# Two attentions of a fused transformer block: the spread reciprocal goes through a PSUM bank, by_block moves to GpSimd, and the first maxima read unstacked halves

## The reference, cut to what matters

```
a = softmax(einsum('bhsd,bhtd->bhst', q, k) * D ** (-0.5))
if causal:
    a = a * (arange(t)[None, :] > arange(s)[:, None])
o = einsum('bhst,bhtd->bhsd', a, v)
```

## Time and profile before

| | us |
|---|---|
| median of 3 runs | 3939.13 (3935.78 to 3939.37) |
| the profiled execution | 3941.99 |
| its span | 3940.2 |
| PE busy | 3361.1 (85%) |
| DVE busy | 2602.9 (66%) |
| ACT busy | 1943.1 (49%) |
| POOL busy | 1420.3 (36%) |

### The profile page before, as it was taken

How to read it: one execution, slowest core, us unless ns; L and a number is a source line. 1 busy time by engine, 2 the same in 40 slices (tenths; PEclk the granted TensorE clock), 3 DMA queues, 4 the chain that set the end, 5 groups by cost and what they waited for, 6 DMA issues and landing times. The chain is left out here.

```text
span 3940.2 us, 64014 instructions
## 1 busy us (share of the span) xinstructions
PE 3361.1 (85%) x22007; PEld 1491.6 (38%) x22007; DVE 2602.9 (66%) x4846; ACT 1943.1 (49%) x3897; POOL 1420.3 (36%) x716
## 2 busy tenths in 40 slices
PE   5999999519885998998989895888889898869998
PEld 2323322307762232322322263222222222657776
DVE  6888885581116778787787355777777773555665
ACT  2777787231112456575566542355555556423443
POOL 2000000452221432414324231366565667506453
PEclk7989998657986999999999796899999999969999
DMA  1000000386752100001000021100000000437445
GB/s 57 14 12 10 12 8 3 148 319 209 227 186 62 32 6 17 13 9 25 5 9 5 24 83 37 31 7 17 14 17 11 8 9 1 128 104 261 89 83 116
DMA packets 163206, 238.92 MB, mean 61 GB/s; under 512 B 35859, under 2 KB 132826, under 8 KB 155994
## 3 DMA queue, kind: packets, MB, share of 16 engines
q1 hardware_dynamic: 142698, 209.40, 16.8%
q0 software_dynamic: 19056, 24.88, 3.5%
q10 hardware_dynamic: 1152, 0.79, 0.1%
HBM read 136.44 MB, written 68.92 MB: 52 GB/s over the span
## 5 line engine op out<-in xcount | busy, mean ns | idle before, releaser
L1254 DVE TENSOR_REDUCE a_part_max<-a_wb 128x1 f32<-128x512 f32 (+1 forms) x2048 | 1164.7, 625 | 268.9 <-PE a_wb L1335 257.8
L1190 ACT ACTIVATE a_e<-a_sc 128x512 f32<-128x512 f32 (+1 forms) x1472 | 796.8, 599 | 785.8 <-PE a_sc L1360 778.3
L1335 PE MATMUL a_wb<-a_ks,a_qs 96*128 96x512 f16 (+1 forms) x2048 | 762.8, 383 | 120.0 <-DVE a_part_max L1254 101.0
L1148 POOL TENSOR_TENSOR a_part_sum<-a_part_sum,a_e 128x2048 f32<-128x2048 f32 x160 | 724.2, 4527 | 185.4 <-ACT a_e L1190 170.0
L1360 PE MATMUL a_sc<-a_qs,a_ks 97*128 97x512 f16 (+1 forms) x1472 | 559.4, 395 | 11.9 <-DMA a_qs<-a_neg_max 8.0
L748 DVE TENSOR_REDUCE xa_part_max<-xa_mx 128x2 f32<-128x802 f32 x512 | 469.7, 985 | 103.8 <-PE xa_mx L845 102.8
L692 ACT ACTIVATE xa_e<-xa_sc 128x512 f32<-128x512 f32 (+1 forms) x832 | 445.7, 596 | 114.2 <-PE xa_sc L832 106.3
L1335 PEld LDWEIGHTS a_wb<-a_ks,a_qs 96*128 96x128 f16 x2048 | 203.2, 99 | 752.0 <-DVE a_part_max L1254 558.8
L1383 PE MATMUL a_po<-a_e,a_v 128*32 128x512 f32 (+1 forms) x2432 | 334.3, 622 | 2.3 <-ACT a_dc L1160 1.2
L1137 POOL TENSOR_TENSOR a_em<-a_e,a_later 128x512 f32<-128x512 f32 x64 | 81.0, 1266 | 590.3 <-issue 371.2
L868 PE MATMUL xa_po<-xa_e,xa_v 128*32 128x256 f32 (+1 forms) x3328 | 274.0, 402 | 7.5 <-ACT xa_oc L735 2.6
(11 more groups left out here) (359 smaller groups left out, 4500.7 us busy)
## 6 DMA issues: line engine op xcount, KB each, us to landing
experts_w_up<-in_we SPq DMA_DIRECT2D x32, 1024.0 KB, 6.2
wall<-expert_halves SPq DMA_DIRECT2D x18, 1088.0 KB, 7.2
experts_w_down<-in_we SPq DMA_DIRECT2D x32, 512.0 KB, 6.3
a_qs<-a_stage SPq DMA_DIRECT2D x360, 32.0 KB, 1.9
moe_xr<-sorted_rows SPq DMA_DIRECT2D x79, 136.5 KB, 2.1
a_ks<-a_stage SPq DMA_DIRECT2D x336, 32.0 KB, 1.9
choose_whole<-in_wm SPq DMA_DIRECT2D x18, 544.0 KB, 9.0
expert_halves<-choose_cut SPq DMA_DIRECT2D x18, 544.0 KB, 7.8
```

The lines of the kernel that those rows point to most:

```text
L1148: pool.tensor_tensor(part_sum[:, :, :], part_sum[:, :, :], tile, ALU.add).then_inc(pool_added, 1)
L1190: act.activation(e[:r, m % ering, j, :], sc[(HG * m + j) % NSC][:r, :], ACT.Exp, scale=scale).then_inc(exp_done, 1)
L1254: dve.tensor_reduce(part_max[:, j, t, k:k + 1], src[:, :mxw], AX.X, ALU.max).then_inc(unit_taken, 1)
L1335: last = pe.matmul(dst[:, :mxw], qs[:STACK, j, n % NQ, P * t:P * t + P], ks[:STACK, g % 2, j, mxs[k]:mxs[k] + mxw], start=True, stop=True)
```

## The change

Four things are edited, all in `attention_stacked`.

- "norm" becomes a numbered unit and gets a `wb` bank: the spread reciprocal is transposed into PSUM, and the multiplication reads it there. PE skips the unit but leaves it the bank.
- In windows with passed tiles, "total" moves to index 20 and "carry" to index 33, and the transposition of `dc` and the addition move from "norm" to "carry". The addition reads the carried sum straight from its bank, and the copy to `divisor` goes.
- `by_block` is written by POOL (`place_sums`), at the fifth tile of the next window.
- The first 16 maxima of window 0 read the high halves in `stage` (32 rows), without the stacking DMAs. Value block 0 stands in the middle of these, block 1 in the middle of the next 16, and blocks 2 and 3 behind the turn.

```diff
@@ -985,12 +985,13 @@
-    before = [("k", 0, 0), ("q", 0), ("k", 0, 1)] + [("v", 0, b) for b in range(nvb)]
+    before = [("k", 0, 0), ("q", 0), ("k", 0, 1)]
     for i in range(nmx):
-        before += maxima(0, [i]) + ([("k", 0, i + 2)] if i + 2 < len(kch) else [])
+        span = maxima(0, [i])
+        before += span[:8] + ([("v", 0, i)] if i < 2 else []) + span[8:] + ([("k", 0, i + 2)] if i + 2 < len(kch) else [])
         if i == 1:
             before.append(("q", 1))
-    before.append(("turn", 0))
+    before += [("turn", 0)] + [("v", 0, b) for b in range(2, nvb)]
...
             work[34:34] = [("norm", n - 1)]
             if passed(n - 1, 0):
-                work[22:22], work[28:28] = [("total", n - 1)], [("carry", n - 1)]
+                work[20:20], work[33:33] = [("total", n - 1)], [("carry", n - 1)]
...
-    number = {u: i for i, u in enumerate(u for u in order if u[0] not in ("total", "norm"))}
+    number = {u: i for i, u in enumerate(u for u in order if u[0] != "total")}
+    ready_at = {u: i for i, u in enumerate(u for u in order if u[0] not in ("total", "norm"))}
...
+            def place_sums(n):
+
+                pool.wait_ge(total_ready, carry_at[n] + 1)
+                if carry_at[n]:
+
+                    pool.wait_ge(unit_ready, ready_at[("carry", max(k for k in carry_at if k < n))] + 1)
+                pool.tensor_tensor(by_block[:, :, :, :],
+                                   total[:, :, :].rearrange("p t j -> p j t").unsqueeze(3).to_broadcast([P, HG, TPC, TPC]),
+                                   in_block[:, :].unsqueeze(1).unsqueeze(1).to_broadcast([P, HG, TPC, TPC]),
+                                   ALU.mult).then_inc(blocks_ready, 1)
+
             for n in range(NC if causal or own_sum else 0):
...
                 for kt in range(nkt):
+                    if kt == TPC and n - 1 in carry_at:
+                        place_sums(n - 1)
...
+            if NC - 1 in carry_at:
+                place_sums(NC - 1)
...
             def carry_sums(n):
 
-                if carry_at[n] == 0:
-                    dve.wait_ge(mask_filled, 5)
+                if carry_at[n]:
+
+                    dve.wait_ge(blocks_ready, carry_at[n])
                 dve.wait_ge(exp_done, HG * (nkt * n + TPC * (n % NCH)))
...
-                dve.tensor_tensor(by_block[:, :, :, :],
-                                  total[:, :, :].rearrange("p t j -> p j t").unsqueeze(3).to_broadcast([P, HG, TPC, TPC]),
...
             def take(u):
-                if u[0] != "norm":
-                    i = number[u]
-                    src = wb[i % NWB]
+                i = number[u]
+                src = wb[i % NWB]
...
-                elif u[0] == "carry":
-                    dve.wait_ge(unit_ready, i + 1)
-                    dve.tensor_copy(divisor[:, :], src[:, :HG * TPC]).then_inc(unit_taken, 1)
-                elif u[0] == "norm":
+                elif u[0] in ("carry", "norm"):
                     n = u[1]
+                    steps = sum(4 if k in carry_at else 3 for k in range(n))
+                    den = turned[:, :].rearrange("p (b r) -> p b r", r=SLOT)[:, :, 0]
+                    if u[0] == "carry" or n not in carry_at:
+                        dve.wait_ge(o_taken, NCOPY * (n + 1))
+                        dve.transpose(turned[:, :], dc[:, :]).then_inc(norm_step, 1)
+                        dve.wait_ge(norm_step, steps + 1)
+                    if u[0] == "carry":
+                        dve.wait_ge(unit_ready, ready_at[u] + 1)
+                        dve.tensor_tensor(divisor[:, :], den, src[:, :HG * TPC], ALU.add).then_inc(norm_step, 1)
+                        dve.wait_ge(norm_step, steps + 2)
+                        dve.sem_inc(unit_taken, 1)
+                        return
...
+                    dve.reciprocal(inverse[:, :], den).then_inc(norm_step, 1)
+                    dve.wait_ge(norm_step, steps + 2)
+                    if i >= NWB:
+
+                        dve.wait_ge(unit_taken, i - NWB + 1)
+                    dve.transpose(src[:, :].rearrange("p (b r) -> p b r", r=SLOT), over(inverse[:, :], SLOT)).then_inc(norm_step, 1)
+                    dve.wait_ge(norm_step, steps + 3)
                     g, o = n // NCH, CH * (n % NCH)
...
-                        dve.tensor_tensor(divisor[:, :], divisor[:, :], den, ALU.add).then_inc(norm_step, 1)
...
-                    dve.transpose(turned[:, :].rearrange("p (b r) -> p b r", r=SLOT), over(inverse[:, :], SLOT)).then_inc(norm_step, 1)
-                    dve.wait_ge(norm_step, steps + 2)
-                    dve.tensor_tensor(ot[:, g, o:o + CH], oc[:, :], turned[:, :], ALU.mult).then_inc(divided, 1)
+                    dve.tensor_tensor(ot[:, g, o:o + CH], oc[:, :], src[:, :], ALU.mult).then_inc(divided, 1)
+                    dve.wait_ge(divided, n + 1)
+                    dve.sem_inc(unit_taken, 1)
...
                     g = n // NCH
-                    if (t, j) == (0, 0):
+                    straight = (n, k) == (0, 0)
+                    if (t, j) == (0, 0) and straight:
+                        pe.wait_ge(split_ready, max(staged[("q", 0)], staged[("k", 0, 0)]) + 1)
+                    elif (t, j) == (0, 0):
                         wait_stacked(pe, ("q", n))
...
+                    if straight:
+                        rows = slice(SLOT * j, SLOT * j + SLOT)
+                        last = pe.matmul(dst[:, :mxw], stage[rows, staged[("q", 0)] % NST, 0, P * t:P * t + P],
+                                         stage[rows, staged[("k", 0, 0)] % NST, 0, :mxw], start=True, stop=True)
+                    else:
+                        last = pe.matmul(dst[:, :mxw], qs[:STACK, j, n % NQ, P * t:P * t + P],
+                                         ks[:STACK, g % 2, j, mxs[k]:mxs[k] + mxw], start=True, stop=True)
```

More of the change, by code:

```diff
@@ L1204, in carry_sums @@
                 dve.wait_ge(total_ready, carry_at[n] + 1)
-                if carry_at[n]:
-                    dve.wait_ge(unit_ready, number[("carry", max(k for k in carry_at if k < n))] + 1)
-                dve.tensor_tensor(by_block[:, :, :, :],
-                                  total[:, :, :].rearrange("p t j -> p j t").unsqueeze(3).to_broadcast([P, HG, TPC, TPC]),
-                                  in_block[:, :].unsqueeze(1).unsqueeze(1).to_broadcast([P, HG, TPC, TPC]),
-                                  ALU.mult).then_inc(blocks_ready, 1)
             def take(u):
-                if u[0] != "norm":
-                    i = number[u]
-                    src = wb[i % NWB]
+                i = number[u]
+                src = wb[i % NWB]
                 if u[0] in "kq":
@@ L1259, in take @@
                     n = u[1]
-                    g, o = n // NCH, CH * (n % NCH)
-                    dve.wait_ge(o_taken, NCOPY * (n + 1))
-                    dve.transpose(turned[:, :], dc[:, :]).then_inc(norm_step, 1)
-                    steps = sum(4 if k in carry_at else 3 for k in range(n)) + 1
-                    dve.wait_ge(norm_step, steps)
-                    den = turned[:, :].rearrange("p (b r) -> p b r", r=SLOT)[:, :, 0]
-                    if n in carry_at:
-                        dve.wait_ge(unit_taken, number[("carry", n)] + 1)
-                        dve.tensor_tensor(divisor[:, :], divisor[:, :], den, ALU.add).then_inc(norm_step, 1)
-                        steps += 1
-                        dve.wait_ge(norm_step, steps)
-                        den = divisor[:, :]
@@ L1272, in take @@
-                    dve.reciprocal(inverse[:, :], den).then_inc(norm_step, 1)
-                    dve.wait_ge(norm_step, steps + 1)
-                    dve.transpose(turned[:, :].rearrange("p (b r) -> p b r", r=SLOT), over(inverse[:, :], SLOT)).then_inc(norm_step, 1)
-                    dve.wait_ge(norm_step, steps + 2)
-                    dve.tensor_tensor(ot[:, g, o:o + CH], oc[:, :], turned[:, :], ALU.mult).then_inc(divided, 1)
+                    steps = sum(4 if k in carry_at else 3 for k in range(n))
@@ new lines, in take @@
+                    if n in carry_at:
+                        den, steps = divisor[:, :], steps + 1
+                    dve.reciprocal(inverse[:, :], den).then_inc(norm_step, 1)
[4 more added lines that the diff above has]
+                    dve.wait_ge(norm_step, steps + 3)
@@ L1334, in unit @@
                                     wait_stacked(pe, ("k", g, c))
-                    last = pe.matmul(dst[:, :mxw], qs[:STACK, j, n % NQ, P * t:P * t + P],
-                                     ks[:STACK, g % 2, j, mxs[k]:mxs[k] + mxw], start=True, stop=True)
+                    if straight:
[5 more added lines that the diff above has]
+                                         ks[:STACK, g % 2, j, mxs[k]:mxs[k] + mxw], start=True, stop=True)
                 elif u[0] == "carry":
```

## The result

| | before | after | ratio (95% interval) |
|---|---|---|---|
| median, us | 3939.25 (4 runs, 3935.78 to 3940.26) | 3850.22 (4 runs, 3843.78 to 3858.91) | 0.9777 (0.9756 to 0.9798) |
| profiled execution: span, us | 3940.2 | 3842.0 | |

The change takes 89 us off the median and 98 us off the profiled execution. The predicted 3820 was 30 us too low; 3850 lies in the range (to 3870), but above the likeliest case's own (3797 to 3845).

What follows compares the result with a forecast made beforehand. PE was taken to set the pace in both loops, DVE close behind. Gaps 68, clock 46, starts 5.5 and ends 1 made 120 us off 3941.99: 3822, given as 3820, with a range to 3870.

Steps and rivals of the forecast that it cites:

- the likeliest case: The whole sum with the clock mostly back: 3797 to 3845 us, chance 0.66.
- The bound, and the multiplication: PE sets the pace in both loops; norm's multiplication, freed of POOL by PSUM, takes 0.69 us: 39.1 us less in a2.
- The bank: At norm, PE can make two maxima instead of three while DVE divides, but goes on a reduction earlier: counted as nothing.
- The chain cut in two: In ten a1 windows, moving transposition and addition to carry shrinks norm's gap from 1.36 to about 0.4 us: 10 us.
- the addition's 9.0: In a1's loop, 10 additions to the divisor fall from 10.9 to 1.9 us: 9.0 us less.
- The clock: In both loops, most PE time at half level outside gaps returns to full: 46 us, between 0 and 63.
- The starts: First reductions come earlier in each attention: 2 us in a1 and 3.5 in a2, together 5.5, between 0 and 9.
- The ends: Behind a1's loop the transposition and the copy leave the last chain: 1 us.
- POOL did not come late: Rival: POOL, inside sums, is late with by_block and PE stands at 12 carries: 3950 us, chance 0.03.
- cover for POOL's sums: Rival: the loops' gaps had let POOL catch up, so half the gain is lost: about 3880 us, chance 0.06.
- the clock would not come back: Rival: remaining gaps in the loops keep bringing half level, clock gain 0 to 20 us: 3845 to 3865, chance 0.2.
- the footing: The sum's 3822 us stood against the profiled execution, 3 us over the median; 3819 on the median's footing, 3820 said.

Runs made afterwards that it cites:

- e1: The changed kernel with the spread reciprocal in SBUF again, so the multiplication has two SBUF inputs: 3915.9 us.
- e2: The kernel before with only the numbered norm and the multiplication reading the spread reciprocal from PSUM: 3878.6 us.
- e9: The changed kernel with the spread reciprocal in SBUF and norm taken out of the count of banks: 3907.8 us.
- e4: The changed kernel with carry directly ahead of norm, so DVE's chain in a1 is whole again: 3857.9 us.
- e5: The changed kernel with two extra transpositions of the inverse in each norm, a longer pause without any lock: 3935.8 us.
- e6: The changed kernel with by_block written by DVE again instead of POOL: 3856.4 us.
- e11: The changed kernel, unchanged, measured once more: 3848.3 us.
- e3: The kernel before with the new start alone (first maxima from unstacked halves, value blocks moved): 3934.9 us.
- e7: The changed kernel with the denominators' transposition and the reciprocal done ahead of norm, or at carry where there is one: 3825.0 us.
- e8: The changed kernel with the queries' projection moved from among the maxima to directly behind norm: 3827.1 us.

## Why the prediction was right, and where it was off

**The bound, and the multiplication.** Right: 0.69 us, least and most alike, with POOL in a sum. e1 shows that nothing else does it. The Trainium skill's rule of the exclusive lock (SBUF — State Buffer, "SBUF: two separate sides"), that a VectorE instruction with two SBUF inputs and GpSimd shut each other out of the ports that they share, agrees: 3294 ns with two SBUF inputs, 687 with one, in otherwise the same program. `a2`'s gaps fell by 35.4 us (34.6 in e2) for the 39.1 forecast. 1.6 us are left at each "norm", the upper of the two values that the prediction worked out, 1.4 and 1.6; the sum was made with the more favourable view that all of DVE's saving reaches PE. The transposition into PSUM cost 727 ns for 711.

**The bank, "I take nothing".** Nearly right: at most some 6 us (e9).

**The chain cut in two, 10 us: the step that failed in the gaps.** `a1`'s gaps fell by 23.4 us, where 29.4 were forecast. e2 and e4 split that: the multiplication gave 7.0 (77.6 to 70.6; forecast 10.4), the other 16.4 (70.6 to 54.2) are there in e4 too (54.1), with the chain whole and the addition out of PSUM (forecast 9.0). The cut is left with less than 1 us of its 10. That the other 16.4 are 7 more than the addition's 9.0 hides most of that loss; this was luck, and what gave the 7 no run shows. The prediction let PE keep 1.97 us of work in hand at "norm", as it had in the earlier trace rows. In after, at the second half of a cut chain (timeline in `a1`):

```profile
1494.15 0.24 DVE L1280 RECIPROCAL a_inverse<-a_divisor 128x16 f32<-128x16 f32 x1
...
1494.52 0.60 PE L1379 MATMUL a_sc<-a_ks,a_qs 97*128 97x512 f16 x2
...
1495.19 0.69 DVE L1288 TENSOR_TENSOR a_ot<-a_oc,a_wb 128x512 f32<-128x512 f32 x1
...
1495.99 0.39 PE L1357 MATMUL a_wb<-a_ks,a_qs 96*128 96x512 f16 x1 [0.88 <-DVEq L1290]
...
1498.29 0.63 PE L1357 MATMUL a_wb<-a_ks,a_qs 96*128 96x512 f16 x1
...
1498.72 0.63 PE L1379 MATMUL a_sc<-a_ks,a_qs 97*128 97x512 f16 x1
```

PE stops at 1495.12, 0.97 us after DVE began, not 1.97. It had spent its banks while DVE made the first half at "carry", and the two maxima between (1.29 us of DVE) don't give them back. So the gap is 0.88, not 0.4, and the cut only deals the same pause out. That the work in hand is what is missing is read from these rows, and e4, with no maxima between the halves and the same pause, agrees; it isn't shown, since the number of banks was not varied.

**The clock, 46 us.** Right in kind, too large by about 14. The loops lost 90.8 us, 58.8 of them gaps (forecast 68), so the clock gave 32. The amount of half level was not misjudged, but its price. The half level fell from 188 to 73 us; outside gaps, where alone it adds time, from 162 to 72 (26 us of before's lay inside gaps; the prediction's estimate for its two stretches was 20). The 46 us, at the half that the prediction allowed at most, stand for 92 us gone. 90 went, and each gave 0.36. Over the 13 profiled executions, a loop without its gaps grows by 0.33 us (`a1`) and 0.41 us (`a2`) for each us at half level outside gaps (a straight line for each loop; the farthest lies 3.2 us off).

Matmuls that follow each other directly do lose nearly half. The stretches around the gap in the rows above:

```profile
1493.00:1496.50 3.50, 2.11 (x7) 0.50 (x6) 3.29 (x6) 3.20 (x12) 0.00 (x0) 1.00 0.00 0
1497.50:1500.50 3.00, 3.00 (x9) 1.00 (x8) 2.88 (x5) 2.71 (x9) 0.00 (x0) 0.50 0.00 0
```

In the first, at full level, the two scores at 1494.52 begin 0.21 us apart (0.60 for both, 0.39 for one). In the second, at half level, the last two rows begin 0.43 us apart, though the record of one maximum only grew from 0.39 to 0.63 us: records overlap, so their length is not the pace. In the loops the loss is smaller. Five executions (after, e1, e5, e6, e11) have the same matmuls in the same order there. Compared place by place, gaps left out, those that ran at half level in one and at full level in another took 293 us at half and 174 at full, so 0.41 of the time was lost (0.44 in `a2`, 0.38 in `a1`); `a1`'s maxima lost 0.44, its scores 0.26 and 0.29. That PE has slack between its scores at full level, which half level uses up, is the likely reason for the smaller price; what it waits for there no run separates.

**The starts, 5.5 us.** 6.0 in the profiles (1.3 and 4.7), 3.0 in e3. `a1`'s first reduction did come 7.1 us sooner after the first key projection (9.9 us instead of 17.0, against the earlier trace rows), and lost it as worked out, behind the two value blocks, near the upper price:

```profile
1231.80 4.87 DVE L1263 TENSOR_REDUCE a_part_max<-a_wb 128x1 f32<-128x512 f32 x8
1239.35 0.69 DVE L1254 COPY a_v<-a_wb 128x512 f32<-128x512 f32 x1 [2.68 <-PE a_wb L1336]
...
1255.95 0.69 DVE L1254 COPY a_v<-a_wb 128x512 f32<-128x512 f32 x1 [2.02 <-PE a_wb L1336]
```

`a2`'s came 10.5 us sooner (6.0 us instead of 16.5), more than the 8.1 worked out, but PE then stood 3.50 us for the stacked second key chunk, and 4.7 us were left at the first score.

**The ends, 1 us.** Nothing: from the last score to the first output matmul -0.3 in `a1`, +0.9 in `a2`.

**The rivals.** POOL did not come late: `by_block` is written long before the fold reads it (timeline of window 4 in `a1`, where the earlier trace rows were).

```profile
1543.27 1.27 POOL L1152 TENSOR_TENSOR a_em<-a_e,a_later 128x512 f32<-128x512 f32 x1 [2.77 <-ACT a_e L1207]
1544.49 0.29 POOL L1133 TENSOR_TENSOR a_by_block<-a_total,a_in_block 128x64 f32<-128x64 f32 x1
```

The fold of that window runs at 1549.54, 4.8 us later. In the loops the gaps were not cover for POOL's sums: POOL's busy time in them is the same within 4 us, in shorter loops, and PE waits for POOL nowhere in `a2`'s loop, before or after, and in `a1`'s for 8.4 us instead of 7.2. That the clock would not come back held in part: of 188 us of half level 73 stayed. The measured 3850 lies inside the range of this rival (3845 to 3865, chance 0.2), 5 us above that of the likeliest case (0.66). By its terms it is nearer to the likeliest case, which had 25 us or more for the clock (32 came, where the rival had 0 to 20); the gaps that fell short and the footing put it over the edge.

**The 30 us.** In the profiles the forecast of 120 is missed by 22: 14 of the clock, 9 of gaps, and small ends of both signs. The other 8 or so are the footing: the profiled execution of after lies 6.4 us below its median, and 3820 had been set 2 us under the sum's 3822.

## What to carry to other kernels

- Where DVE shares its time with long POOL instructions, look at the spread of each DVE instruction with two SBUF inputs, not at its least: moving one operand to PSUM took the multiplication from 3.5 to 0.69 us here, and a small addition from 1.09 to 0.18.
- A pause of PE that half level follows costs more than its length (1.5 times from before to after, 2.1 times in e5), so price gaps and half level together; but leave out the half level that lies inside gaps, and take the rest at what such loops lost by it (0.33 to 0.41 us for each us here), not at a half.
- A chain cut in two gained nothing here, where the engine that waits could not build up work between the halves (read from rows, not tested by itself); moving what doesn't need the bank ahead (e7), or giving PE work of its own at that place (e8), gained 25 and 23 us, and both together (3820) no more than that, as far as can be told.

## What was not expected of the hardware

- The length of a matmul's record misleads on the clock: the 512-column maximum took 0.63 us at half level for 0.39 at full, but the starts of neighbours lay 0.43 us apart for 0.21. The loops lost less than a half, 0.33 to 0.41 us for each us at half level outside gaps.
- The same pauses don't always bring half level: two executions of one program had 51 and 68 us at half level in the same loop, with gaps of 54 and 52 us. What decides it was not settled.
- Half level costs time of its own, beside the gaps: e8 took only 5.3 us of gaps away but 43 us of half level, and was 20 us shorter in the loops.
